# Edge stage of a two-layer graph network: when a gather of sender rows may start, and which semaphore it raises

## The reference, cut to what matters

```python
s, v = node_feats[:, :32] @ W_up_s, node_feats[:, 32:] "@" W_up_v     # per node
w = silu(silu(edge_feats @ A1 + b1) @ A2 + b2) @ A3                   # per edge, four weights of 32
ss, vs = s[sender], v[sender]                                         # rows gathered by sender
mji = concat(ss*y_s*w0, sum_i(vs*y_v)*w3, ss*y_v*w1, vs*y_s*w2)       # 256 values per edge
message = segment_sum(mji, receiver, 6250)                            # then W_out, residual, layer norm
```

## Time and profile before

| what | value |
|---|---|
| runs | 2175.22, 2174.67, 2174.66 us; median 2174.67 |
| span of the profiled execution | 2710.9 us |
| edge stage in it, first gather to the last matmuls | 1339 to 2711 us |
| PE busy, of the span | 79% |
| POOL busy, of the span | 58% |
| granted PE clock, mean | 0.875 |

### The profile page before, as it was taken

How to read it: one execution, slowest core, us unless ns; L and a number is a source line. 1 busy time by engine, 2 the same in 40 slices (tenths; PEclk the granted TensorE clock), 3 DMA queues, 4 the chain that set the end, 5 groups by cost and what they waited for, 6 DMA issues and landing times.

```text
span 2710.9 us, 32629 instructions
## 1 busy us (share of the span) xinstructions
PE 2142.9 (79%) x10173; PEld 1641.3 (61%) x10173; DVE 1597.6 (59%) x3607; ACT 1490.2 (55%) x4706; POOL 1585.6 (58%) x1673
## 2 busy tenths in 40 slices
PE   6688888888888888888777777777778777877776
PEld 4567666776777767677555555555555555555554
DVE  4567566656666666666645545555555555555555
ACT  4545455445555555555366655656566656665655
POOL 5466666666666666665355555555556655655553
PEclk8899899899999999998778888778877888888888
DMA  6566666665665666565211111111111111112111
GB/s 236 170 195 183 193 206 188 181 173 171 178 180 170 181 173 180 170 178 152 67 40 46 45 41 44 43 41 45 45 39 47 46 41 46 47 40 75 41 42 41
DMA packets 118698, 299.97 MB, mean 111 GB/s; under 512 B 29058, under 2 KB 42604, under 8 KB 118524
## 3 DMA queue, kind: packets, MB, share of 16 engines
q0 software_dynamic: 90912, 263.36, 34.7%
q1 hardware_dynamic: 27612, 34.51, 3.8%
HBM read 278.50 MB, written 19.26 MB: 110 GB/s over the span
## 4 chain that ended last, share of the span: by engine, by line
ACT 21%; another core or an unknown queue 13%; PE 9%; issue 7%; DVE 1%; ACTq 0%; DVEq 0%
ACT bank L984 20%; PE bank L928 4%; PE bank L896 2%; PE bank L877 1%; PE bank L884 1%; ACT h L972 0%; ACT h L964 0%; PE bank L907 0%; PE bank L908 0%; DVE side L1029 0%; DVE msg L1032 0%; DVE msg L1030 0%; DVE y_high L1072 0%; PE bank L903 0%
## 5 line engine op out<-in xcount | busy, mean ns | idle before, releaser
L862 POOL DMA_INDIRECT sender<-table,src_index x832 | 784.8, 943 | 585.9 <-DVE msg L1040 303.3
L318 POOL DMA_INDIRECT shared<-gates,seq_index x784 | 742.1, 947 | 447.0 <-issue 207.6
L984 ACT ACTIVATE bank<-bank,attr 128x64 f32<-128x64 f32 x3328 | 702.2, 373 | 1.1 <-PE bank L896 0.5
L562 ACT ACTIVATE bank<-bank,bias 128x512 f32<-128x512 f32 (+1 forms) x624 | 375.7, 633 | 452.8 <-PE bank L396 329.2
L386 PE MATMUL bank<-ident,shared 128*128 128x128 f32 x3136 | 466.1, 292 | 173.3 <-DVE h_lo L700 135.0
L386 PEld LDWEIGHTS bank<-ident,shared 128*128 128x128 f32 x3136 | 396.9, 151 | 260.2 <-DVE h_lo L700 166.1
L928 PE MATMUL bank<-msg,select 128*128 128x256 f32 x1664 | 512.1, 453 | 1.2 <-DVE msg L1040 1.2
L1029 DVE TENSOR_TENSOR side<-sender,bank 128x192 f32<-128x192 f32 x416 | 146.6, 352 | 553.0 <-ACT bank L984 401.4
L896 PEld LDWEIGHTS bank<-a,h 64*128 64x128 f32 x1664 | 239.3, 219 | 349.6 <-issue 222.7
L896 PE MATMUL bank<-a,h 64*128 64x128 f32 x1664 | 282.6, 319 | 156.6 <-ACT bank L984 111.9
L928 PEld LDWEIGHTS bank<-msg,select 128*128 128x128 f32 x1664 | 349.0, 224 | 74.9 <-issue 7.4
(11 more groups left out here) (119 smaller groups left out, 2389.8 us busy)
## 6 DMA issues: line engine op xcount, KB each, us to landing
sender<-table,src_index POOLq DMA_INDIRECT x832
gates<-shared SPq DMA_DIRECT2D x49, 256.0 KB
shared<-gates,seq_index POOLq DMA_INDIRECT x784
feats<-attr_in SPq DMA_DIRECT2D x13, 256.0 KB
x<-x_t_in SPq DMA_DIRECT2D x12, 256.0 KB
table<-up SPq DMA_DIRECT2D x12, 256.0 KB, 2.3
out<-shared SPq DMA_DIRECT2D x9, 256.0 KB
shared<-x_t_in SPq DMA_DIRECT2D x3, 704.0 KB, 9.8
```

The costliest lines, as they stand in the source:

```text
L318: pool.indirect_dma_start(out=rows[:, k % SLOTS, j, :], out_offset=None, in_=t["gates"], in_offset=bass.IndirectOffsetOnAxis(ap=seq_index[ ...
L562: act_e.activation(candidate[:, k % 2, 0:width] if gate == 2 else values, values, ACT.Tanh if gate == 2 else ACT.Sigmoid, bias=bias2[:, ga ...
L862: pool.indirect_dma_start(out=sender[:, hg % 4, j, :], out_offset=None, in_=t["table"], in_offset=bass.IndirectOffsetOnAxis(ap=src_index[: ...
L984: last = act_e.activation(wy[:, j, :, k, :], w[:, 2 * i + j, :, min(k, 1), :], ACT.Copy, scale=attr[:, k, tile:tile + 1])
```

## The change

A gather of tile k waits, from the third on, until the gather of tile k-2 has landed. For that each of the 16 places has a semaphore of its own, `e_gather[hg % 4][j]`, raised by 16 per use. DVE waits for the four semaphores of a half group in place of one. The list of semaphores to be cleared for a second pass grows accordingly.

```diff
--- before.py
+++ after.py
@@ -814,14 +814,14 @@
 
         e_rel, e_turn = sem("e_rel"), sem("e_turn")
         e_feats = [sem("e_feats0"), sem("e_feats1")]
-        e_gather = [sem(f"e_gather{i}") for i in range(4)]
+        e_gather = [[sem(f"e_gather{i}_{j}") for j in range(HALF)] for i in range(4)]
         e_p1, e_h1, e_p2, e_h2, e_w, e_scaled = (sem(n) for n in ("e_p1", "e_h1", "e_p2", "e_h2", "e_w", "e_scaled"))
         e_sel, e_msg, e_half, e_acc = (sem(n) for n in ("e_sel", "e_msg", "e_half", "e_acc"))
         e_side, e_free, e_next = (sem(n) for n in ("e_side", "e_free", "e_next"))
         f_turn, f_copy, f_proj, f_sum, f_st, f_mom = (sem(n) for n in (
             "f_turn", "f_copy", "f_proj", "f_sum", "f_st", "f_mom"))
         f_sqrt, f_rstd, f_norm, f_out, f_base = (sem(n) for n in ("f_sqrt", "f_rstd", "f_norm", "f_out", "f_base"))
-        e_sems = [e_rel, e_turn, *e_feats, *e_gather, e_p1, e_h1, e_p2, e_h2, e_w, e_scaled,
+        e_sems = [e_rel, e_turn, *e_feats, *e_gather[0], *e_gather[1], *e_gather[2], *e_gather[3], e_p1, e_h1, e_p2, e_h2, e_w, e_scaled,
                   e_sel, e_msg, e_half, e_acc, e_side, e_free, e_next,
                   f_turn, f_copy, f_proj, f_sum, f_st, f_mom, f_sqrt, f_rstd, f_norm, f_out, f_base]
         mlp_bank, weight_bank, scaled_bank, acc_bank = banks[0], banks[1:3], banks[3:5], banks[5:7]
@@ -859,10 +859,13 @@
                             pool.wait_ge(e_msg, hg - 3)
                         for j in range(HALF):
                             tile = hg * HALF + j
+                            if tile >= 2:
+                                before, place = divmod(tile - 2, HALF)
+                                pool.wait_ge(e_gather[before % 4][place], 16 * (before // 4 + 1))
                             pool.indirect_dma_start(
                                 out=sender[:, hg % 4, j, :], out_offset=None, in_=t["table"],
                                 in_offset=bass.IndirectOffsetOnAxis(ap=src_index[:, tile:tile + 1], axis=0),
-                            ).then_inc(e_gather[hg % 4], 16)
+                            ).then_inc(e_gather[hg % 4][j], 16)
 
                 @block.tensor
                 def _(pe):
@@ -1033,7 +1036,8 @@
                                           ALU.mult).then_inc(e_free, 1)
 
                     def messages(hg):
-                        dve.wait_ge(e_gather[hg % 4], 16 * HALF * (hg // 4 + 1))
+                        for j in range(HALF):
+                            dve.wait_ge(e_gather[hg % 4][j], 16 * (hg // 4 + 1))
                         products(2 * hg)
                         products(2 * hg + 1)
                         dve.wait_ge(e_side, 2 * hg + 2)
@@ -1165,7 +1169,7 @@
                         pool.tensor_tensor(rel[:], rel[:], wrap[:], ALU.mult).then_inc(e_next, 1)
                         pool.wait_ge(e_next, 13)
 
-                        pool.dma_reset(range(e_gather[0].num, e_gather[3].num + 1))
+                        pool.dma_reset(range(e_gather[0][0].num, e_gather[3][HALF - 1].num + 1))
                         for s in e_sems:
                             pool.sem_clear(s)
```

## The result

The change takes 2428.2 us (median of 4 runs, 2426.5 to 2429.9) where the kernel before took 2174.7 on the same chip (2171.6 to 2175.2): a ratio of 1.117, 95% interval 1.1157 to 1.1184, or 253.6 us more. The forecast was slower, 2332 us, in a range of 2190 to 2440.

A forecast was written before the change was run, and what follows sets the result against it. POOL's issue of gathers was taken as the bound, 5.00 us per half group; the landing wait makes it 5.76, so 204 x 0.76 = 155 plus 2 gives 157 us: 2174.7 + 157 = 2332 us, range 2190 to 2440.

The forecast's parts named there:

- POOL's pace: Edge stage: POOL issues gathers 1.25 us apart, 5.0 us per half group; 832 gathers are 1040 us, 48% of the median.
- the 504 us of POOL's waits: POOL's idle time in the profile, 303 us edge stage plus some 201 us LSTM stage, taken as absent outside the profile.
- the last step of the prediction: Profile after the change: the span rises far less than the median, to 2710 to 2800 us.
- upper bound: Edge stage with late landing and dear restart: 6.44 us per half group, 294 us more, 2469 us.
- Landing: Edge-stage gather, start to landing: 2.5 us taken, from a span of 2.24 to 2.64 us.
- Rival 1: Edge-stage gathers land within 2.24 us of their start: time stays 2174.7 us, or 2224 with a 0.5 us restart; chance 0.14.
- The riding wait: POOL, edge stage: a wait carried by the gather itself restarts it 0.26 us after the landing.
- The separate wait: POOL, each half group's first gather: two waits, one its own instruction; restart 0.26 to 0.9 us, 0.5 taken.
- DVE's waits: DVE, edge stage: four waits for one per half group, up to 0.9 us, covered by DVE waiting for POOL; nothing taken.
- Rival 2: Edge stage not POOL's outside the profile: hold-ups at 5.5 us per half group, cost 53 us, 2228 us; chance 0.06.
- Rival 3: POOL's queue empties each time, every edge gather pays the 0.9 us restart: 374 us more, 2548 us; chance 0.04.
- Rival 4: PE's clock drops to 1.2 GHz in the edge stage's pauses: some 265 us more, 2440 us; chance 0.04.

## Why the prediction was right, and where it wasn't

**POOL's pace.** Right for the runs that were compared, and shown: 832 gathers in 1039 us in the profile of the semaphores alone, and the 253 us of added gaps are the whole difference. The argument, that the 504 us of POOL's waits must be absent from a median of 2175, held. What I made of it did not: I laid the pauses to the profiled execution against the runs. They belong to some of the chips, whatever runs there. Therefore the last step of the prediction, a span of 2710 to 2800 us after, failed on both kinds: 2428 without pauses, 2684 with. And the 504 us are not quite even: I took the ordinary gaps out of the LSTM stage's waits and left them in the edge stage's 303.3 us (85 of 0.30, 26 us).

**The size.** The mechanism held, but the cost is 254 us where the sum gave 157, and the measured time lies 12 us inside the upper end of the range. That end, 2440, is worked out nowhere for the forecast's own mechanism (its upper bound was 2469), so that the range held is in part luck. Where the 97 us are can be read gather by gather in the trace of the change, which has 780 of the 832 landings. From a half group's first gather to its third it takes 2.91 us in the mean (2.76 taken), from there to the next first 3.31 us (3.00 taken).

**Landing.** 2.5 us from the start taken, 2.5 us shown as the median. Rival 1, a landing in time, is out: no landing took under 2.4 us. The Trainium skill's "DMA: Bandwidth & Descriptors", section "Anatomy of one DMA — SWDGE (gpsimd) path", puts such a DMA at about 2.0 us plus its bytes at 436 GB/s, an estimate of 2.15 us for this size. These gathers' 2.5 us don't agree with that, and the measurement decides.

**The riding wait.** 0.26 us taken, 0.26 us in the chain; right.

**The separate wait.** This is the term that was mis-sized: "I take 0.5", against 0.74 in the chain and in the steps of 3.24 us, near the upper of my two ends, 0.9. I set the row of the program's first gather aside as cold; but for 0.2 us it was the right row. 0.24 x 204 = 49 us of the 97 missing.

**Late landings.** I worked with one landing time and named no tail. The two landings of a half group that POOL waits for last take 2.56 and 2.62 us in the mean, 0.18 us over the 5.00 taken: 0.18 x 204 = 37 us. About half of it is a tail, with 42 of the 780 above 2.8 us and the latest here:

```profile
2175.81 5.32 DMA sender<-table,src_index
```

Some restarts of over 0.26 and 0.74 us bring another 8 us, and 3 are left.

**DVE's waits, the clearing list, the LSTM stage.** Nothing, as predicted; shown by the ratio of 1.0002.

**The rivals.** Rival 2 describes the chips with pauses, but from the wrong side: on the one where the change ran it costs nothing and gains 3.3%, and to a gain I gave 0.02. Rival 3, a restart ahead of every gather, is out (0.30 ahead of half of them). Rival 4 is out as a cost: the granted clock of the stage fell from 0.98 to 0.88, and PE was busy for 993 us of it in place of 863, and yet POOL's gaps account for all of the time.

**What stays open.** Why some chips pause, and why the edge stage stops pausing at 6.2 us per half group and not at 5.8; the two were seen on different chips. The views show that ACT waits for a matmul that by its row has long ended; that holding POOL back is what takes the pauses away, or that less work of PE per us is, was not told apart. The gain there was seen on one chip, and the kernel before has no profile from that chip. Beside the 1321 and 1345 us of the other profiles the stage's 1291 would explain 30 to 54 us, and the runs differ by 94.

## What to carry to other kernels

Where an engine that issues gathers is the pace, a wait for a landing costs the landing plus a restart less the distance; here the second last was 0.3 us too near where the wait rides and 0.8 where it doesn't, the third last cost 0.8%, and a semaphore for each place alone cost nothing. If two waits stand ahead of one instruction, write first the one that will end last, so that it rides: 65 to 80 us here. And when span and median differ by a fifth, ask whether the same kernel has two times on two chips before the profiler is blamed, and time a change on both kinds.

## What was not expected of the hardware

The kernel before takes 2174 to 2176 us in three comparisons and 2704 and 2779 us on two other chips; in the profile from the first of these ACT pauses for up to 9.8 us ahead of the same two lines. A change that costs 11% on the first kind gains 3.3% on the second of these chips. And a wait on POOL costs 0.74 us as an instruction of its own, 0.26 as a part of the gather behind it.
